# A weights stage dissolved into a line recurrence, and the recurrence written out without loops

## The reference, cut to what matters

```
def _pass_fwd(out, w, b, axis):            # out: (8, 64, 32, 32); w: (64, 64, 9)
    rows = moveaxis(out, axis, 0)
    step(carry, x): new = x + relu(conv1d(carry, w, b))      # 9 taps, padding 4
    res = [rows[0], scan(step, rows[0], rows[1:])]
def _pass_bwd(out, w, b, axis): the same from the last line back to line 1
out = _pass_fwd(x,   w_d, b_d, axis=2)     # vertical, down:   31 steps
out = _pass_bwd(out, w_u, b_u, axis=2)     # vertical, up:     30 steps
out = _pass_fwd(out, w_r, b_r, axis=3)     # horizontal, right: 31 steps
out = _pass_bwd(out, w_l, b_l, axis=3)     # horizontal, left:  30 steps
```

## Time and profile before

| | us |
|---|---|
| median of 3 runs | 1483.65 (1482.17 to 1483.76) |
| span of the profiled execution | 1477.3 |
| non-local stage and before it | 0 to about 199 |
| weights stage | about 199.3 to 219.0 |
| vertical passes | about 219.3 to 335.4 |
| horizontal passes | about 335.7 to 457.5 |
| all that follows | about 458 to 1477.3 |

### The profile page before, as it was taken

One profiled execution on the slowest core, in us unless ns is written; L12 is line 12 of the kernel. 1 busy time (PEld: TensorE's weight loads), 2 busy tenths in 40 slices (PEclk: granted clock), 3 DMA queues, 4 the chain that ended last, 5 costly groups with the idle time before them and its releaser, 6 DMA issues. The chain is left out here.

```text
span 1477.3 us, 31682 instructions
## 1 busy us (share of the span) xinstructions
PE 1340.9 (91%) x12866; PEld 856.7 (58%) x12866; DVE 606.5 (41%) x942; ACT 589.5 (40%) x1029; POOL 163.2 (11%) x178
## 2 busy tenths in 40 slices
PE   8999978888987999998899999999999999948767
PEld 5323357777776788887555555555555555536544
DVE  4981131111113677775432332333333333335652
ACT  3986742225576455454422222222222222223440
POOL 4000019600002222221000000000000000003000
PEclk9879979999998899999999999999999999979977
DMA  4900000000005000000000000000000000040001
GB/s 108 115 1 1 1 4 0 0 0 0 0 0 198 33 4 4 4 4 3 1 0 0 0 0 0 0 0 0 0 0 0 0 0 0 0 115 1 1 1 58
DMA packets 34319, 24.19 MB, mean 16 GB/s; under 512 B 24653, under 2 KB 28781, under 8 KB 34237
## 3 DMA queue, kind: packets, MB, share of 16 engines
q1 hardware_dynamic: 33853, 21.92, 6.7%
q10 hardware_dynamic: 384, 1.07, 0.3%
HBM read 20.80 MB, written 2.18 MB: 16 GB/s over the span
## 5 line engine op out<-in xcount | busy, mean ns | idle before, releaser
L1130 PE MATMUL sp_f<-hankel,sp_ut 128*128 x2304 | 420.9, 344 | 0.0
L1130 PEld LDWEIGHTS sp_f<-hankel,sp_ut 128*128 128x128 f16 x2304 | 222.8, 98 | 216.7 <-issue 27.5
L1169 ACT COPY sp_sums<-sp_f 64x1023 f32<-64x1023 f32 x128 | 129.0, 1008 | 426.7 <-PE sp_f L1130 426.7
L1192 DVE COPY sp_sums<-sp_f 64x1024 f32<-64x1024 f32 x128 | 155.3, 1213 | 91.8 <-PE sp_f L1130 91.8
L1190 DVE COPY sp_mix<-mix 128x512 f32 x64 | 27.3, 427 | 280.7 <-PE sp_f L1130 280.7
L1141 PE MATMUL sp_o<-sp_sums,sp_mix 128*64 128x128 f32 (+2 forms) x1024 | 123.6, 392 | 0.0
L502 PE MATMUL convv<-runningv,toeplitz 128*128 128x128 f32 x610 | 85.7, 287 | 15.1 <-DVE runningv L519 15.1
L502 PEld LDWEIGHTS convv<-runningv,toeplitz 128*128 128x128 f32 x610 | 74.2, 191 | 26.6 <-DVE runningv L519 26.6
L502 PE MATMUL convh<-runningh,toeplitz 128*128 128x128 f32 x610 | 84.0, 284 | 4.5 <-DVE runningh L519 1.3
L1141 PEld LDWEIGHTS sp_o<-sp_sums,sp_mix 128*64 128x64 f32 x1024 | 63.2, 134 | 37.4 <-issue 15.4
L502 PEld LDWEIGHTS convh<-runningh,toeplitz 128*128 128x128 f32 x610 | 74.0, 191 | 13.3 <-DVE runningh L519 13.3
(11 more groups left out here) (311 smaller groups left out, 1888.3 us busy)
## 6 DMA issues: line engine op xcount, KB each, us to landing
hankel<-phi_rows SPq DMA_DIRECT2D x32, 256.0 KB, 6.5
ex_w<-in_L_ffn_weight SPq DMA_DIRECT2D x1, 2080.0 KB
m_plus<-in_L_ffn_M_phi_plus SPq DMA_DIRECT2D x2, 1024.0 KB, 14.2
m_minus<-in_L_ffn_M_phi_minus SPq DMA_DIRECT2D x2, 1024.0 KB, 16.5
out<-x SPq DMA_DIRECT2D x8, 256.0 KB, 3.4
x<-in_x ACTq DMA_DIRECT2D x2, 512.0 KB, 7.6
x<-in_x SPq DMA_DIRECT2D x2, 512.0 KB, 9.0
ar<-in_L_ffn_M_u SPq DMA_DIRECT2D x2, 192.0 KB, 3.5
```

The lines of the kernel that those rows point to most:

```text
L1130: mm = nc.tensor.matmul(f_ps[b][:, lo:(half + 1) * BANK], ut[:, hu, b, i, :, :].rearrange("p a c -> p (a c)"), m.hankel[:, hf, ds(j * 2 + ...
L1169: nc.scalar.copy(sums[n][HALF[1], b, 1:T], f_ps[b][HALF[1], 0:T - 1]).then_inc(f_act, 1)
L1192: nc.vector.tensor_copy(sums[n][HALF[0], b, :], f_ps[b][HALF[0], :]).then_inc(f_dve, 1)
```

## The change

`weights_stage` is gone as a stage. A class `LateWeights` holds its tensors and its pieces of work, and `conv_passes` takes it as `beside` (the vertical passes alone; the horizontal ones have none). Ahead of step 1 ACT pads the first weights, PE turns them and ACT takes the first tap table. All other pieces stand behind given steps n of the recurrence, on each engine after what that step does there:

- PE: phi behind steps 1, 2 (4 transposes each); Wu behind 3, 4 (4 each); Wq with Wk behind 5 to 8 (4 matmuls, 8 passes each); tap table 2 behind 9, 10 (6 and 4 transposes); Wv with Wu behind 12 to 15 (8 passes each), and the filter gain behind 14; tap tables 3 and 4 behind 17, 18 and 22, 23.
- ACT: square roots behind 3 and 4, padding behind 6, 13, 19, the exponential behind 8, tap tables taken behind 11, 20, 25.
- DVE: the chain on phi behind 3 to 9, the copies of products behind 10, 11, 17, 18, the softmax behind 1 and 12, the gain behind 15.
- POOL: the masks, then a wait for DVE's softmax, then the mixing as before. SP: the store of phi's rows inside the vertical block.

The loops of `conv_passes` are written out: all 61 steps of both directions stand in the code with constant addresses and counts. The core of the diff:

```diff
-        def steps(eng, step):
-            step(1, 1, first)
-            with eng.Fori(1, (FWD + 1) // 2) as k:
-                for odd in range(2):
-                    step(k * 2 + odd, odd, first)
...
             @block.tensor
             def _(pe):
+                if beside is not None:
+                    beside.tensor_first(pe)
+                for n in range(1, FWD + BWD + 1):
+                    odd = n % 2
                     pe.wait_ge(fetch_ok, n)
-                    if not isinstance(n, int):
+                    if n > 1:
                         pe.wait_ge(line_ok, n - 1)
                     nc.tensor.matmul(conv[odd][:, :, :], m.ident[:, :], added[odd][:, :, :], start=True, stop=False)
+                    if beside is not None:
+                        beside.taps_ready(pe, n, FWD)
                     pe.wait_ge(line_ok, n)
...
                     mm.then_inc(conv_ok, 1)
+                    if beside is not None:
+                        beside.tensor(pe, n)
...
+                for n in range(1, FWD + BWD + 1):
+                    odd, wn = n % 2, taps_of(n)
+                    if n > 1:
                         dve.wait_ge(saved, n - 1)
                     dve.wait_ge(conv_ok, n)
                     nc.vector.scalar_tensor_tensor(...).then_inc(line_ok, 1)
+                    if beside is not None:
+                        beside.vector(dve, n)
...
+                if beside is not None:
+                    beside.scalar_first(act)
+                fetch(1)
+                fetch(2)
+                for n in range(1, FWD + BWD + 1):
...
+class LateWeights:
+    def tensor_first(self, pe):
+        pe.wait_ge(self.m.w_in, 16 * LOADS)
+        pe.wait_ge(self.edges, 2)
+        pe.wait_ge(self.pad_ok, 1)
+        self.turn_taps(0, range(SHIFTS)).then_inc(self.turned_ok, 1)
+    def taps_ready(self, pe, n, fwd):
+        if n == 1:
+            pe.wait_ge(self.taken, 1)
+        if n == fwd + 1:
+            pe.wait_ge(self.taken, 2)
+    def scalar_first(self, act):
+        act.wait_ge(self.m.w_in, 16 * LOADS)
+        self.pad_taps(0).then_inc(self.pad_ok, 1)
+        act.wait_ge(self.turned_ok, 1)
+        self.take_taps(0).then_inc(self.taken, 1)
...
-            weights_stage(nc, m, raw, phi_rows)
-            vertical_passes(nc, m, mixing_step)
+            vertical_passes(nc, m, raw, phi_rows, mixing_step)
```

More of the change, by code:

```diff
@@ L464, in nonlocal_stage, with conv_passes @@
             extra(block)
-def conv_passes(nc, m, lines, first, tag, extra):
+def conv_passes(nc, m, lines, first, tag, extra, beside=None):
     LINES = H
@@ L480, in inner, with line_of, taps_of @@
             return tile[:, :, PADP:PADP + PAIRS]
[L482 to L490 removed]
+        def line_of(n):
+            return n if n <= FWD else 2 * FWD - n
+        def taps_of(n):
+            return first if n <= FWD else first + 1
         with nc.Block() as block:
@@ L536, in _ @@
[L536 to L554, removed]
+                def fetch(n):
+                    back, line = n > FWD, line_of(n)
+                    (lines.refetch if back else lines.fetch)(nc.scalar.copy, added[n % 2][:, :, :], line // 2, line % 2).then_inc(fetch_ok, 1)
@@ new lines, in _ @@
+                if beside is not None:
+                    beside.scalar_first(act)
+                fetch(1)
+                fetch(2)
+                for n in range(1, FWD + BWD + 1):
+                    line = line_of(n)
+                    act.wait_ge(line_ok, n + 1)
+                    (lines.store if n > FWD else lines.keep)(nc.scalar.copy, inner(running[n % 2]), line // 2, line % 2).then_inc(saved, 1)
+                    if n in (FWD - 1, FWD):
+                        act.wait_ge(saved, n + 1)
+                    if n + 2 <= FWD + BWD:
+                        fetch(n + 2)
+                    if beside is not None:
+                        beside.scalar(act, n)
@@ new lines, in pad_taps, with take_taps, turn_taps @@
+    def pad_taps(self, n):
+        return self.nc.scalar.copy(self.padded[:, n, 1:TAPS + 1, :], self.raw.conv[HALF[n // 2], n % 2, :].rearrange("o (i k) -> o k i", k=TAPS))
+    def take_taps(self, n):
+        return self.nc.scalar.copy(self.m.toeplitz[:, n, :, :], self.turned[:, :, :, :].rearrange("p s a c -> p s (a c)"))
+    def turn_taps(self, n, some):
+        for s in some:
+            for po in range(2):
+                first = 2 * s - po + 1
+                mm = self.nc.tensor.transpose(self.turned[:, s, po, :], self.padded[:, n, first:first + 2, :].rearrange("o t i -> o (t i)"), self.m.ident[0:C, 0:C])
+        return mm
@@ L1830, in _, with spectral_mixing @@
+def spectral_mixing(nc, m, block, step, weights):
     @block.gpsimd
```

334 lines of the change are left out of this document (183 added, 151 removed).

## The result

| | us |
|---|---|
| before, median of 4 runs | 1482.91 (1479.17 to 1483.76) |
| after, median of 4 runs | 1466.09 (1462.41 to 1467.33) |
| ratio, 95% interval | 0.9899 (0.9877 to 0.992) |
| after, profiled execution | 1465.79, span 1464.1 |
| predicted | 1468.5 (1461 to 1476) |

The kernel is 16.8 us faster between the medians, 15 by the ratio; the forecast was 15.1. Spans first: 1477.3 before, 1464.1 after, 13.2 less. The stretch on which the change acts can be cut at five instants that both traces have, and the cut shows where the time went.

What follows compares the result with a forecast made beforehand. Bound: no engine full in the weights stage, then a PE to DVE to PE chain in the vertical passes. Vertical -13.2 and horizontal -1.9 give -15.1 on 1477.3, so 1462.2, plus 6.35 is 1468.5 us; range 1461 to 1476.

Steps and rivals of the forecast that it cites:

- Front: Start of the new block to the first tap load: at 203.4 instead of 220.06, 16.7 us earlier.
- Cold steps: Vertical steps 1 and 2, clock back to full after 4.5 us: 2.3 us lost, between 1.3 and 4.5.
- Extras on PE: PE's pieces beside the vertical steps at full clock, each barely fitting: cost 1.0 us, bounds 0 and 11.2.
- Rival B: PE's pieces in the vertical passes do not hide, small ones paid in full: +4.8 us, 1473.3; chance 0.14.
- The prediction's own sign of being wrong: Vertical steps 3 to 23 together taking over 6 us more than 21 x 1.89 = 39.7.
- Other engines: DVE, ACT, POOL and SP work beside the vertical steps: cost 0, or 0.5 us once or twice.
- Loops: Recurrence steps written out, all with two DVE waits: 1.89 us each, 113.4 over 60 vertical steps.
- Rival A: In the recurrence the 0.06 us is the loop's, not the second wait's; steps take 1.83: 1462.2 us; chance 0.20.
- Sum over the vertical passes: First tap load to that of step 61: 113.4 + 2.3 + 1.0 = 116.7 us.
- the way out: First direction of the horizontal passes: 15 odd steps lose 0.06 us each, +0.9.
- the way back: Horizontal return, ACT starting sooner with constant addresses: pairs of 3.82 us instead of 4.01, -2.8, bounds 0 and -4.5.
- Around the span: Time outside the profiled span, median less span: 6.35 us, added to 1462.2 to give 1468.5.

Runs made afterwards that it cites:

- the last experiment: Changed kernel with DVE's two waits swapped, tap tables turned in four, four and two transposes, nine extra 128x128 matmuls at the block's start; 1458.59 us, ratio 0.9846.

## Why the prediction was right, point by point

**Front: right.** 4.1 us from the stage's start to the first tap load predicted, 4.11 measured. (The prediction's terms add to 201.86 for ACT's copy of the taps, not to its 201.92; the 0.06 is too little to matter.) The four durations out of the earlier trace rows came back as 1.22, 1.36, 0.69 and 0.38, and no other engine took the place of the one removed.

**Cold steps: right in kind, too dear.** 2.3 us were taken. Step 1 took 207.56 - 204.22 = 3.34 from tap load to tap load (3.46 predicted), and step 2 took 1.90, nothing lost: the clock was back 3.2 us after the first tap load, not 4.5. The term is 1.4. The value of the earlier trace rows for before, full by 3.4 us, would have given it; the allowance for phi's transposes between was unfounded. Nor is "so long after the first tap load" the right measure: in the last experiment it was 1.7 us. That allowance leaned the way of the rule in the Trainium skill, TensorE: Matmul & The Clock Gate, Part 4: PE-mode transpose, that transposes do not count as PE being busy. By that rule they might have put off the return; here four of them stood in the stretch and did not.

**Extras on PE: right sum, with errors that cancel.** 1.0 predicted, 1.0 by the law; but the 1.0 was chosen between wide bounds and not added up, so that it came out to the tenth is in part luck. An eight-pass piece is 0.31 of loads and 0.38 of slot, where 0.40 was used. Six transposes are 0.51, where 0.38 was used, so those steps lost 0.15 each instead of fitting; the gain matmul lost 0.34 instead of 0.2. The change of kind, feared at 0.17 twice a step, does cost: 0.21, once a step, on the way into the piece. It did not show because PE's room was 0.57, not the 0.41 to 0.48 of its idle time. Rival B asked for 5.8. (Its base, 11.5 us of PE time without phi at half clock, is a little low: the stage's weight loads are 12.93, of which phi has 0.8.) The prediction's own sign of being wrong was 6 us over 39.7 for steps 3 to 23: from DVE of step 3 to that of step 24 it is 41.3.

**Other engines: right.** Cost 0 predicted, and every step behind the first is the longer of 1.90 and the law's value, but for the stall and 0.06 at the turn. ACT's store behind the square roots' table load comes 0.04 late and the one behind the exponential 0.2, where 0.5 to 0.7 was feared. POOL is idle for 30.65 us ahead of its next work at 323.46, as "over 30" said.

**Loops: right.** Steps of 1.89 to 1.90 from the second wait, not from the loop. The experiment with the swapped waits sharpens the cause: it is the order of the waits, and the trace of before had it already, with a semaphore instruction for the late wait 0.07 ahead of each even step of DVE (0.18 on the horizontal way back) and none ahead of the odd ones. The prediction called this a place for the 0.06 by the Trainium skill, Perfetto Trace Analysis, Identifying Dependency Chains, which says that such an instruction may get semaphore instructions ahead of it; the runs agree that they are there and cost 0.07 us a step when the late wait sits on them. Rival A named 1.83 a step as what would come of written-out loops alone; the written-out loops alone gave 1.90.

**Sum over the vertical passes.** 116.77 from first to last tap load: 60 steps of 1.897 are 113.8, cold 1.4, extras 1.0, the stall at 19 to 20 0.4. Predicted 113.4 + 2.3 + 1.0 = 116.7. The 0.9 too much for the cold steps paid for the stall and the rounding of 1.89.

**Horizontal: the way out right, the way back right by luck.** Out +1.05 (+0.9 predicted), back -3.3 (-2.8). On the way back the pair takes 3.80 (3.82 predicted), and ACT starts 0.38 behind DVE as taken from the earlier trace rows. But the chain through ACT that the prediction added up is not what sets the time. With swapped waits the same stores and the same fetch run in steps of 1.83, so at 1.90 the chain of DVE and PE sets it here too, as on the way out. Nor does the prediction's sum close on the kernel before: with ACT's old start it is 0.35 + 0.11 + 1.61 + 1.83 = 3.90, not the 4.01 measured. It took ACT's part from the wrong step of the pair. These rows of before show the one that holds the chain up:

```profile
401.81 0.35 DVE L519 SCALAR_TENSOR_TENSOR runningh<-convh,conv_bias,addedh 128x128 f32<-128x128 f32 x1 [1.85 <-PE convh L502]
...
402.30 1.23 ACT L609 COPY x<-runningh 64x64 f32 x4 [0.67 <-DVE runningh L519]
403.56 0.30 ACT L601 COPY addedh<-cols 128x128 f32 x1
...
403.99 0.19 PEld L499 LDWEIGHTS convh<-addedh,ident 128*128 128x128 f32 x1 [0.58 <-DVE runningh L519]
```

ACT starts 0.49 behind DVE, the identity matmul stands 1.69 later, and with the 1.83 the pair is 4.01. (The last row names DVE as the releaser, but it had ended only 0.01 before, where PE follows DVE's end by 0.05 in the earlier trace rows, and the code has this matmul wait for an older line; the fetch, ended at 403.86, fits.) Only ACT's start brought down to 0.38 would have made it 3.90, 1.7 us less over 15 pairs instead of 2.8. The stores and the fetch got shorter as well (421.45 to 423.06 is 1.61), ACT left the chain, and the waits' 1.90 happens to be half of the 3.82 that was forecast, within 0.01.

**Not predicted: the change of direction.** 1.25 us went between the last vertical and the first horizontal step. Before, the clock fell there, after it did not. The trace of before, then that of the kernel with the loops written out:

```profile
337.00:338.00 1.00, 1.00 (x6) 1.00 (x6) 0.00 (x0) 0.41 (x2) 0.00 (x0) 0.50 0.00 0
```

```profile
341.00:342.00 1.00, 1.00 (x7) 1.00 (x6) 0.00 (x0) 0.39 (x1) 0.00 (x0) 0.54 0.00 0
```

PE's weight loads pause for 2.16 to 2.50 us there in each kernel. Over the nine traces the clock fell in four (those two, the doubled product, the smaller pieces), each time for 3.4 us, and stayed in five. It cost 1.1 to 1.3 us in three of them; in the kernel with only the loops written out it was 1.6, of which 0.3 are a longer pause. Since it goes both ways among kernels that hold the dissolved stage, it isn't shown to be an effect of the change; the profiled executions put it into the difference of the spans. What decides it stays open.

**Around the span.** The prediction read 6.35 us around the span of before. Every run of the changed kernel has 1.7 (1465.79 on 1464.1). So the profiled execution of before was a faster one, near 1479 (one of its four runs took 1479.17), and not at the median. Since the same number was added on both sides it did not move the forecast of the difference.

## What to carry to other kernels

Work that has to be done once can leave the path of a recurrence if it is cut to the idle slot that PE has in a step: measure the time PE needs for the step itself with nothing waiting, with the change into the piece (1.54 here), subtract it from the step (1.90), and cut pieces to that (0.36). Where an instruction waits on two events, write the one that comes late so that the step's own instruction holds it (here: first). For one moved line that was worth 7.2 us in the passes, nearly half of what the whole restructuring brought there. And loops with registers cost nothing here on PE and DVE, which idle in every step; on ACT, which stood in the chain on the horizontal way back, they did (a pair of steps 4.01 against 3.80). So look at which waits and register instructions stand ahead of which instruction in each form.

## What the runs showed of the hardware

- A semaphore instruction released by the late event costs 0.07 us before the instruction behind it starts (1.55 against 1.48 of DVE's idle time in every plain step).
- Behind the ten passes of the taps a load of the same kind follows 1.11 us after their start, one of 64 rows 1.32: 0.21 us for the change. Phi's transposes, of 128 rows, followed at 1.12 in the kernel with filler (205.31 to 206.43). With it counted, 1.54 + slot holds to 0.01 us for slots of 0.38 to 2.34.
- The step's instruction behind a released semaphore instruction came 0.43 to 0.44 us behind it instead of 0.07 once each in five of the kernels, in four of them at step 20 of the vertical passes.
- Passes of 64x64 matmuls that alternate between the two halves of the output partitions took 0.03 us each at full clock ((0.54 - 0.31) / 8), those that stayed in one half, with the same operands each time, 0.06 (a group of 32 in 1.94 us). At half clock eight alternating passes took 0.81, so the ratio of the two clocks alone would give 0.40 for what took 0.31.
- Between the same instructions the granted clock can stay full over a pause of 2.2 to 2.5 us of PE or fall (five and four of nine traces). Where it fell at the change of direction it stood at half for 3.4 us in all four. At the start of the vertical passes it was 6.8 us in five kernels with the dissolved stage, 3.4 in one, none in one, and 23.9 us in both kernels that hold the weights stage in one piece.
